# Making the decayed inputs of a state-space scan on VectorE from PSUM instead of on GpSimd from SBUF

## Chip, cores, metric

The kernel runs on one core of a Trainium2 chip. The metric is the device time of one launch in microseconds; the time before is the median of three runs.

## What is computed

The reference is one block of two layers on 2048 tokens of width 512: a Mamba-2 layer (chunked state-space scan, 16 heads of 64 channels, state 128) and a mixture of 8 experts. The change touches only the scan. Cut to what matters, per chunk of tokens:

```python
xdt = xc * dtc[..., None]                       # x scaled by its time step, per head
CB = einsum('bclgn,bcsgn->bcgls', Cc, Bc)
Y_diag = einsum('bcgls,bgHcls,bcsgHp->bclgHp', CB, Lmat, xdt)
decay_states = exp(dA_cs[..., -1:] - dA_cs)     # per head and token
states = einsum('bcsgn,bgHcs,bcsgHp->bcgHpn', Bc, decay_states, xdt)
# then the carry over chunks, Y_off, gate, RMS norm, output projection
```

The product `decay_states * xdt` under the last einsum is what the kernel calls `xdd`.

## The kernel before

The kernel has three stages on all engines: a front (router, decays; up to about 100 us), the experts, and, from about 285 us, the scan. The scan works on 16 tiles of 128 tokens, t = 0 to 15, in 8 groups of two tiles. Here an even tile is the first of its group (`c == 0`), an odd tile the second. Beside the tiles of group g, the engines compute the input projection, convolution and gate of group g + 1 in nine slices (`stage_pe`, `stage_act`, `stage_dve`), of which four lie in the even tile and five in the odd one. The last group (tiles 14 and 15) has no such slices beside it. All engines run a program in fixed order and meet by semaphores.

What a tile does, in the order of each engine:

- **TensorE** transposes B into `pk` (line 1631) and x into `pxb[0]`, `pxb[1]` (line 1635; each 128x512), multiplies C by B (`pk`, line 1639), runs the output projection of the tile before (`po`, line 1595), then the column sum of its squares (`pk`, line 1600, which waits for the third step of GpSimd's sum), then `py` from the carry (line 1616), the diagonal product `py<-m,xdt` (line 1623), and the new state `pxb<-xdd,btok` (line 1657), which waits for `xdd`. Slices of the next group (`pi`, line 1343) lie in between.
- **VectorE** makes `xdt` from the transposed x in PSUM, in two halves (line 1496), `cbm` (line 1503, after TensorE's line 1639), multiplies the decay kernel `m` by it (line 1506, 128x2048), then computes `cst` and `dec` of the next tile (lines 1446 and 1449), the residual (lines 1546 to 1555), convolution taps (line 1299), `var`, the products with `e` (line 1469), `y` (line 1478) and the carry (line 1535).
- **ScalarE** takes exponentials of `dec` and `cd` (lines 1362, 1363) as soon as VectorE's `dec` is there; behind them in its order stand a quarter of the next decay kernel (line 1370) and the squares of the finished tile (line 1386).
- **GpSimd** makes `xdd` from `xdt` and `dec` (line 1228), sums the squares of the tile before in three steps (lines 1208, 1210, 1212, after ScalarE's squares), issues two gathers (lines 1236, 1241), makes `rstdy` (line 1218), scales the carry (line 1249), and adds and gates `y` (lines 1254, 1257).

`xdd` is made in GpSimd's order directly ahead of the sum of squares:

```python
pool.wait_ge(xdt_done, t * 2 + 2 + CR)
pool.wait_ge(dec_done, t + 1 + CR)
pool.wait_ge(st, t + CR)
pool.tensor_tensor(xdd[:, :, :, :], xdt[:, :, :, :], dec[c]..., ALU.mult).then_inc(xdd_done, 1)
```

Of the kernel before, what the change touches and what calls it, by code (L numbers as in the profile page):

```python
# [18 lines left out]
ALU = mybir.AluOpType  # L19
# [8 lines left out]
P = 128  # L28
TOKENS, D = 2048, 512
KD = D // P  # L30
INNER, STATE, HEADS, HD, TAPS = 1024, 128, 16, 64, 4
XB = INNER // P
# [3 lines left out]
T = TOKENS // P  # L36
# [103 lines left out]
CR = 1  # L140
# [43 lines left out]
def static(i, *values):  # L184
    return isinstance(i, int) and i in values
# [754 lines left out]
def mamba(nc, low, over, late, wraw, whl, wo, xh0, smalls, hooks, sem, x, w_in, w_out_in, conv_w_in, conv_b_in,  # L940
# [5 lines left out]
    with ExitStack() as ctx:  # L946
        def pb(name, shape):
            return ctx.enter_context(nc.psum_tensor(name, shape, F32))
# [3 lines left out]
        xdt = over("xdt", [P, XB, 2, HD])  # L952
        xdd = over("xdd", [P, XB, 2, HD])
# [12 lines left out]
        dec = [late(f"dec{i}", [P, HEADS]) for i in range(2)]  # L966
        cd = [late(f"cd{i}", [P, HEADS]) for i in range(2)]
        var = late("var", [P, 1])
        rstd = late("rstdy", [P, 1])
        pwt = late("pwt", [P, 2])  # L970
        sidx = late("sidx", [P, 2], U32)
        carry = low("carry", [P, XB, 2, HD])
        e2 = low("e2", [P, XB, P])
# [7 lines left out]
        pxb = [pb(f"pxb{i}", [P, 4, P]) for i in range(2)]  # L981
# [18 lines left out]
        res_in = sem("res_in")  # L1000
        ya_in = [sem(f"ya_in{i}") for i in range(2)]
        sidx_done = sem("sidx_done")
        sidx_ready = sem("sidx_ready")
        pw_done = sem("pw_done")
        ra_done = sem("ra_done")
# [3 lines left out]
        inz_free = sem("inz_free")  # L1009
        halo = sem("halo")  # L1010
        tap = sem("tap")
        ctap = sem("ctap")
        txd = sem("txd")
        xs_done = sem("xs_done")
# [3 lines left out]
        xdt_done = sem("xdt_done")  # L1018
        cst_done = sem("cst_done")
        dsub = sem("dsub")  # L1020
        dec_done = sem("dec_done")
# [4 lines left out]
        cbm_done = sem("cbm_done")  # L1026
        m_done = sem("m_done")
        xdd_done = sem("xdd_done")
        st = sem("st")
        yoff = sem("yoff")  # L1030
        ydiag = sem("ydiag")
        ye = sem("ye")
        yd = sem("yd")
        cdec = sem("cdec")
        cadd = sem("cadd")
        yadd = sem("yadd")
        ygate = sem("ygate")
# [6 lines left out]
        var_done = sem("var_done")  # L1044
        rstd_done = sem("rstd_done_m")
        res_done = sem("res_done")
        o_done = sem("o_done")
# [83 lines left out]
        def groups(eng, body):  # L1131

            by_twos(eng, G, lambda g, par, r: body(g, par))
# [56 lines left out]
            sp.wait_ge(o_out, 16 * T + 16)  # L1190

        def gpsimd(pool):
            for s in (yadd, ygate, xdd_done, cdec, rstd_done):
                pool.sem_inc(s, CR)
            pool.sem_inc(tree, 3)
            pool.memset(nhalf[:, :], -0.5).then_inc(nh_done, 1)
            pool.wait_ge(nh_done, 1)
            pool.wait_ge(down, J + CR)
            pool.wait_ge(y_done, J + CR)
            pool.wait_ge(h_lo, J + 2)  # L1200
            pool.wait_ge(w_lo, NP)
            for i in range(2):
                pool.wait_ge(y_out[i], 16 * ((J + 1 - i) // 2) + 16)

            def sums(t):

                pool.wait_ge(ysqd, t + 1 + CR)
                pool.tensor_tensor(ysq[:, 0:4, :], ysq[:, 0:4, :], ysq[:, 4:8, :], ALU.add).then_inc(tree, 1)  # L1208
                pool.wait_ge(tree, t * 3 + 4)
                pool.tensor_tensor(ysq[:, 0:2, :], ysq[:, 0:2, :], ysq[:, 2:4, :], ALU.add).then_inc(tree, 1)  # L1210
                pool.wait_ge(tree, t * 3 + 5)
                pool.tensor_tensor(ysq[:, 0:1, :], ysq[:, 0:1, :], ysq[:, 1:2, :], ALU.add).then_inc(tree, 1)

            def factor(t):

                pool.wait_ge(var_done, t + 1 + CR)
                pool.wait_ge(o_done, t + CR)
                pool.tensor_tensor(rstd[:, :], var[:, :], nhalf[:, :], ALU.pow).then_inc(rstd_done, 1)

            def body(g, par):  # L1220
                for c in range(2):
                    t = g * 2 + c
                    first = static(t, 0)
                    if not static(t, T - 1):
                        pool.wait_ge(xdt_done, t * 2 + 2 + CR)
                        pool.wait_ge(dec_done, t + 1 + CR)
                        pool.wait_ge(st, t + CR)
                        pool.tensor_tensor(xdd[:, :, :, :], xdt[:, :, :, :],  # L1228
                                           dec[c][:, :].rearrange("p (a b) -> p b a", a=2).unsqueeze(3)
                                           .broadcast_to([P, XB, 2, HD]), ALU.mult).then_inc(xdd_done, 1)  # L1230
                    if not first:
                        sums(t - 1)

                    if not first:
                        pool.wait_ge(res_done, t + CR)
                    pool.tensor_copy(sidx[:, :], slot_u[:, :, bass.ds(t, 1)].rearrange("p k t -> p (k t)")  # L1236
                                     ).then_inc(sidx_done, 1)
                    pool.wait_ge(sidx_done, t + 1)
                    pool.sem_inc(sidx_ready, 1)
                    for n in range(2):  # L1240
                        pool.indirect_dma_start(ya[n][:, :], None, y_d, bass.IndirectOffsetOnAxis(ap=sidx[:, n:n + 1], axis=0)  # L1241
                                                ).then_inc(ya_in[n], 16)
                    if not first:
                        factor(t - 1)
                    if static(t, T - 1):
                        return
                    pool.wait_ge(yoff, t * 2 + 2 + CR)
                    pool.wait_ge(cadd, t * 2 + CR)
                    pool.tensor_tensor(carry[:, :, :, :], carry[:, :, :, :],
                                       cd[c][:, :].rearrange("p (a b) -> p b a", a=2).unsqueeze(3)  # L1250
                                       .broadcast_to([P, XB, 2, HD]), ALU.mult).then_inc(cdec, 1)
                    pool.wait_ge(yd, t * 2 + 2 + CR)
                    pool.wait_ge(ye, t * 2 + 2 + CR)
                    pool.tensor_tensor(y[:, :, :], y[:, :, :], e2[:, :, :], ALU.add).then_inc(yadd, 1)  # L1254
                    pool.wait_ge(yadd, t + 1 + CR)
                    pool.wait_ge(inz_free, g * NZ + NZ + CR)
                    pool.tensor_tensor(y[:, :, :], y[:, :, :], zs[par][:, :, c * P:(c + 1) * P],  # L1257
                                       ALU.mult).then_inc(ygate, 1)

            groups(pool, body)  # L1260
            sums(T - 1)
            factor(T - 1)
# [164 lines left out]
            square(T - 1)  # L1427

        def vector(dve):
            for s in (inz_free, xs_done, xdt_done, cbm_done, m_done, ye, yd, cadd, var_done, o_done, ctap, res_done):  # L1430
                dve.sem_inc(s, CR)
            dve.sem_inc(o_out, 16)
            for n in LAST:
# [23 lines left out]
            def body(g, par):  # L1457
                for c in range(2):
                    t = g * 2 + c
# [34 lines left out]
                    for half in range(2):  # L1494
                        dve.wait_ge(xtr, t * 2 + half + 1)
                        dve.tensor_tensor(  # L1496
                            xdt[:, 4 * half:4 * half + 4, :, :],
                            pxb[half][:, :, :].rearrange("p b (a d) -> p b a d", a=2),
                            dt_tok[:, bass.ds(t, 1), :].rearrange("p t (a b) -> p (t b) a", a=2)
                            [:, 4 * half:4 * half + 4, :].unsqueeze(3).broadcast_to([P, 4, 2, HD]),  # L1500
                            ALU.mult).then_inc(xdt_done, 1)
                    dve.wait_ge(cbt, t + 1)
                    dve.tensor_tensor(cbm[:, :], pk[:, 1, :], tri[:, :], ALU.mult).then_inc(cbm_done, 1)
                    dve.wait_ge(me, t + 1 + CR)
# [58 lines left out]
            def finish(t):  # L1563
# [6 lines left out]
                                         op0=ALU.mult, op1=ALU.add).then_inc(o_done, 1)  # L1570

            groups(dve, body)
            residual(T - 1)
            variance(T - 1)
            finish(T - 1)

        def tensor(pe):
# [88 lines left out]
            project(T - 1)  # L1666

        return {"sync": sync, "gpsimd": gpsimd, "scalar": scalar, "vector": vector, "tensor": tensor}


# [51 lines left out]
```

## Time and profile before

| | before |
|---|---|
| median of 3 runs | 766.76 us (764.72 to 768.8) |
| the profiled execution, its own time | 762.99 us |
| its span, first to last instruction | 760.9 us |
| TensorE busy | 657.8 us (86%) |
| VectorE busy | 513.5 us (67%) |
| ScalarE busy | 376.9 us (50%) |
| GpSimd busy | 329.8 us (43%) |
| mean granted TensorE clock | 0.971 |

Busy shares are over the whole span, three stages with different limits; what an edit is worth has to be read in the stretch in which it lies. The span leaves out some 2 us of the execution's own time at its two ends. Start times in the rows are counted from the span's start. "Idle before, releaser" says how long the engine stood ahead of an instruction and what ended that.

### The profile page before, as it was taken

How to read it: one execution, taken by the hardware profiler on the slowest of the kernel's cores; microseconds unless marked ns; L12 is line 12 of the kernel's file. 1: busy time of each engine (PE TensorE's matmuls, PEld its weight loads, DVE VectorE, ACT ScalarE, POOL GpSimd, SP SyncE). 2: the span in 40 equal slices, each digit the busy share in tenths (PEclk: the TensorE clock that was granted, in tenths of full speed). 3: DMA queues.
4: the chain of work that ended last, by engine and by line, in shares of the span. 5: the costliest groups of instructions: out<-in, count | busy, mean ns of one | idle time of the engine just before them, and what ended most of it. 6: DMA issues, size and time to landing. Idle time of an engine off the chain costs nothing.

```text
span 760.9 us, 13663 instructions
## 1 busy us (share of the span) xinstructions
PE 657.8 (86%) x4201; PEld 542.1 (71%) x4202; DVE 513.5 (67%) x987; ACT 376.9 (50%) x773; POOL 329.8 (43%) x305
## 2 busy tenths in 40 slices
PE   3970139999999988789999999999999999999765
PEld 3970128898998778776786786787777777777442
DVE  7339474434444467588788788788788787797464
ACT  1243313444544465767456556556555565654410
POOL 4208952223222100235564564555546546546451
PEclk9999959999999998999999999999999999999898
DMA  9992024644655613321342343243233233224121
GB/s 317 369 393 102 1 62 134 200 140 122 174 168 168 250 56 139 97 79 61 112 139 65 103 139 96 70 137 110 69 124 110 82 111 113 68 96 138 56 61 36
DMA packets 36062, 96.39 MB, mean 127 GB/s; under 512 B 5376, under 2 KB 9216, under 8 KB 33856
## 3 DMA queue, kind: packets, MB, share of 16 engines
q1 hardware_dynamic: 28304, 67.96, 25.8%
q0 software_dynamic: 7728, 28.05, 13.0%
q8 instruction: 16, 0.26, 0.1%
q14 instruction: 14, 0.11, 0.1%
HBM read 73.06 MB, written 22.94 MB: 126 GB/s over the span
## 4 chain that ended last, share of the span: by engine, by line
PE 58%; POOL 14%; issue 12%; DVE 8%; ACT 3%; DMA 3%; SPq 0%; POOLq 0%; DVEq 0%; ACTq 0%
PE pi L1343 19%; PE pg L877 9%; PE pd L888 6%; PE po L1595 5%; PE py L1616 4%; PE prt L648 3%; PE py L1623 3%; PE px L862 2%; POOL y L1254 2%; DVE y L1478 2%; PE pt L642 2%; POOL ysq L1208 2%; PE pxb L1657 2%; POOL xdd L1228 2%; DVE xs L1299 2%
## 5 line engine op out<-in xcount | busy, mean ns | idle before, releaser
L1343 PE MATMUL pi<-xh,whl 128*128 128x256 f32 x1152 | 166.9, 288 | 9.0 <-ACT raw L1274 4.6
L1343 PEld LDWEIGHTS pi<-xh,whl 128*128 128x128 f32 x1152 | 148.3, 191 | 13.4 <-issue 7.1
L1299 DVE SCALAR_TENSOR_TENSOR xs<-raw,conv_w,xs 128x256 f32<-128x256 f32 x240 | 119.6, 567 | 4.1 <-ACT xs L1277 4.1
L1595 PE MATMUL po<-wo,y 128*128 128x512 f32 x256 | 114.6, 601 | 1.4 <-POOL y L1257 0.9
L1343 PE MATMUL pi<-xl,whl 128*128 128x256 f32 x576 | 92.9, 284 | 0.0
L1595 PEld LDWEIGHTS po<-wo,y 128*128 128x128 f32 x256 | 48.3, 194 | 56.7 <-issue 55.3
L1370 ACT ACTIVATE m<-m,cst 128x128 f32<-128x128 f32 x256 | 79.4, 388 | 0.5
L1343 PEld LDWEIGHTS pi<-xl,whl 128*128 128x128 f32 x576 | 79.0, 191 | 0.0
L877 PE MATMUL pg<-ew,xgh 128*128 x312 | 65.3, 352 | 0.0
L1254 POOL TENSOR_TENSOR y<-y,e 128x1024 f32<-128x1024 f32 x15 | 35.8, 2388 | 65.2 <-DVE y L1478 65.2
L1208 POOL TENSOR_TENSOR ysq<-ysq 128x512 f32<-128x512 f32 x16 | 22.8, 1423 | 86.8 <-ACT ysq L1386 79.7
L1228 POOL TENSOR_TENSOR xdd<-xdt,dec 128x1024 f32<-128x1024 f32 x15 | 29.1, 1939 | 64.8 <-DVE xdt L1496 64.8
L877 PEld LDWEIGHTS pg<-ew,xgh 128*128 128x128 f32 x312 | 53.6, 192 | 0.1
L769 POOL DMA_INDIRECT xg<-xn_d,ic x39 | 38.9, 998 | 30.7 <-POOL ic L766 30.7
L1280 ACT ACTIVATE zs<-pi 128x512 f32<-128x512 f32 x32 | 19.1, 598 | 63.2 <-PE pi L1343 63.2
L1506 DVE TENSOR_TENSOR m<-m,cbm 128x2048 f32<-128x2048 f32 x16 | 47.6, 2976 | 1.7
L1241 POOL DMA_INDIRECT ya<-y_d,sidx x32 | 40.2, 1257 | 18.0 <-POOL sidx L1236 13.1
L888 PE MATMUL pd<-ew,hh 96*128 x156 | 45.9, 416 | 0.5 <-issue 0.5
L831 DVE SCALAR_TENSOR_TENSOR hg<-th,pg 128x192 f32<-128x192 f32 x39 | 13.8, 353 | 46.7 <-ACT th L789 46.7
L1277 ACT ACTIVATE xs<-raw,conv_b,conv_w 128x256 f32<-128x256 f32 x80 | 43.8, 594 | 1.3
L766 POOL COPY ic<-idx 128x1 uint32 (+1 forms) x39 | 9.2, 237 | 80.5 <-PE px L862 80.5
L840 DVE TENSOR_TENSOR hl<-ph,hh 96x256 fp32r<-96x256 f32 x39 | 16.4, 421 | 38.1 <-ACT hh L795 21.2
(180 smaller groups left out, 1278.6 us busy)
## 6 DMA issues: line engine op xcount, KB each, us to landing
m<-cs_d SPq DMA_DIRECT2D x16, 1024.0 KB, 4.7
y_d<-yo SPq DMA_DIRECT2D x39, 256.0 KB
e<-cs_d SPq DMA_DIRECT2D x32, 256.0 KB, 4.0
ew<-in_w_gu POOLq DMA_DIRECT2D x8, 768.0 KB, 16.1
xin<-in_x SPq DMA_DIRECT2D x8, 512.0 KB, 7.2
xn_d<-xin SPq DMA_DIRECT2D x8, 512.0 KB, 23.2
xt_d<-ew SPq DMA_DIRECT2D x8, 512.0 KB, 17.2
xl<-xt_d SPq DMA_DIRECT2D x8, 512.0 KB, 4.0
```

The lines of the kernel that those rows point to most:

```text
L769: pool.indirect_dma_start(xg[par][:, :], None, xn_d, bass.IndirectOffsetOnAxis(ap=ic[par][:, 0:1], axis=0)).then_inc(xg_in[par], 16)
L877: mm = pe.matmul(pg[par][:, :], xx[par][:, k, :], of(ww, e, k), start=n == 0, stop=n == 11)
L888: mm = pe.matmul(pd[par][:, :], xx[par][:, k, :], of(ww, e, k), start=n == 0, stop=n == 5)
L1228: pool.tensor_tensor(xdd[:, :, :, :], xdt[:, :, :, :], dec[c][:, :].rearrange("p (a b) -> p b a", a=2).unsqueeze(3) .broadcast_to([P, XB, ...
L1241: pool.indirect_dma_start(ya[n][:, :], None, y_d, bass.IndirectOffsetOnAxis(ap=sidx[:, n:n + 1], axis=0)).then_inc(ya_in[n], 16)
L1254: pool.tensor_tensor(y[:, :, :], y[:, :, :], e2[:, :, :], ALU.add).then_inc(yadd, 1)
L1277: act.activation(xs[par][:, b, :], raw[:, b, 0:GT], ACT.Identity, bias=conv_b[:, b:b + 1], scale=conv_w[:, b, 0:1]).then_inc(tap, 1)
L1299: dve.scalar_tensor_tensor(out=xs[par][:, b, :], in0=raw[:, b, k:k + GT], scalar=conv_w[:, b, k:k + 1], in1=xs[par][:, b, :], op0=ALU.mult ...
L1343: mm = pe.matmul(pi[n % 2][:, h, :], whl[:, n, lo, k, h * P:(h + 1) * P], xx[:, k, :], start=k3 == 0, stop=k3 == 11)
L1370: act.activation(m[c][:, h, :], m[c][:, h, :], ACT.Relu, bias=cst[c][:, h:h + 1], scale=-1.0).then_inc(seg, 1)
L1506: dve.tensor_tensor(m[c][:, :, :], m[c][:, :, :], cbm[:, :].unsqueeze(1).broadcast_to([P, HEADS, P]), ALU.mult).then_inc(m_done, 1)
L1595: mm = pe.matmul(po[:, :], y[:, b, :], wo[:, b, :], start=b == 0, stop=b == XB - 1)
```

## The change

The factor `dtd` (128x16) is `dec` times the time step, made by one small VectorE instruction. `xdd` is then the transposed x in PSUM times `dtd`, in two instructions of 128x512 on VectorE, between `xdt` and `cbm`. GpSimd's multiplication goes, and with it its three waits. The products are made for tiles 0 to 14, as before. VectorE now waits for ScalarE's `dec` of this tile (`dec_done`) and for its own `dtd` (`dtd_done`).

```diff
@@ gpsimd
-                    if not static(t, T - 1):
-                        pool.wait_ge(xdt_done, t * 2 + 2 + CR)
-                        pool.wait_ge(dec_done, t + 1 + CR)
-                        pool.wait_ge(st, t + CR)
-                        pool.tensor_tensor(xdd[:, :, :, :], xdt[:, :, :, :],
-                                           dec[c][:, :].rearrange("p (a b) -> p b a", a=2).unsqueeze(3)
-                                           .broadcast_to([P, XB, 2, HD]), ALU.mult).then_inc(xdd_done, 1)
@@ vector, after the two xdt instructions
+                    if not static(t, T - 1):
+                        dve.wait_ge(dec_done, t + 1 + CR)
+                        dve.tensor_tensor(dtd[:, :], dec[c][:, :], dt_tok[:, bass.ds(t, 1), :].rearrange("p t h -> p (t h)"),
+                                          ALU.mult).then_inc(dtd_done, 1)
+                        dve.wait_ge(dtd_done, t + 1)
+                        for half in range(2):
+                            ins = dve.tensor_tensor(
+                                xdd[:, 4 * half:4 * half + 4, :, :],
+                                pxb[half][:, :, :].rearrange("p b (a d) -> p b a d", a=2),
+                                dtd[:, :].rearrange("p (a b) -> p b a", a=2)
+                                [:, 4 * half:4 * half + 4, :].unsqueeze(3).broadcast_to([P, 4, 2, HD]), ALU.mult)
+                        ins.then_inc(xdd_done, 1)
                     dve.wait_ge(cbt, t + 1)
                     dve.tensor_tensor(cbm[:, :], pk[:, 1, :], tri[:, :], ALU.mult).then_inc(cbm_done, 1)
```

On VectorE, in the loop's odd tile, before (`pxb0`, `pxb1` are the halves of the transposed x, `m1` is this tile's decay kernel; ISA and REGISTER_ALU carry waits and counters):

```order
L1493 ISA
L1496 REGISTER_ALU [waits xtr_m,ydiag]
L1496 TENSOR_TENSOR xdt_146<-pxb0,dt_tok_52 128x512
L1495 REGISTER_ALU
L1496 ISA [waits xtr_m]
L1496 TENSOR_TENSOR xdt_146<-pxb1,dt_tok_52 128x512
L1503 TENSOR_TENSOR cbm_158<-pk,tri_50 128x128 [waits cbt]
L1504 REGISTER_ALU
L1506 TENSOR_TENSOR m1_145<-m1_145,cbm_158 128x2048 [waits cbm_done,me]
L1442 ISA
L1446 ISA [waits xdd_done,me,bc_in0]
```

and now:

```order
L1491 TENSOR_TENSOR xdt_146<-pxb0,dt_tok_52 128x512
L1490 REGISTER_ALU
L1491 ISA [waits xtr_m]
L1491 TENSOR_TENSOR xdt_146<-pxb1,dt_tok_52 128x512
L1498 REGISTER_ALU
L1499 TENSOR_TENSOR dtd_168<-dec1_162,dt_tok_52 128x16 [waits dec_done]
L1503 TENSOR_TENSOR xdd_147<-pxb0,dtd_168 128x512 [waits dtd_done]
L1503 TENSOR_TENSOR xdd_147<-pxb1,dtd_168 128x512
L1510 TENSOR_TENSOR cbm_158<-pk,tri_50 128x128 [waits cbt]
L1513 TENSOR_TENSOR m1_145<-m1_145,cbm_158 128x2048 [waits cbm_done,me]
L1437 ISA
L1441 ISA [waits xdd_done,me,bc_in0]
```

Three instructions came between the second `xdt` and `cbm`, so `cbm`, `m`, `cst` and `dec` all stand behind them.

On GpSimd, in the loop, from the gate of an even tile (`zs1`) to the sum of squares in the odd tile behind it, before:

```order
L1256 ISA [waits yadd]
L1257 TENSOR_TENSOR y_148<-y_148,zs1_156 128x1024 [waits inz_free]
L1225 ISA
L1226 REGISTER_ALU [waits xdt_done]
L1228 TENSOR_TENSOR xdd_147<-xdt_146,dec1_162 128x1024 [waits st,dec_done]
L1208 TENSOR_TENSOR ysq_149<-ysq_149 128x512 [waits ysqd]
L1209 ISA
L1210 TENSOR_TENSOR ysq_149<-ysq_149 128x256 [waits tree]
```

and now:

```order
L1251 ISA [waits yadd]
L1252 TENSOR_TENSOR y_148<-y_148,zs1_156 128x1024 [waits inz_free]
L1210 TENSOR_TENSOR ysq_149<-ysq_149 128x512 [waits ysqd]
L1211 ISA
L1212 TENSOR_TENSOR ysq_149<-ysq_149 128x256 [waits tree]
L1213 REGISTER_ALU
L1214 TENSOR_TENSOR ysq_149<-ysq_149 128x128 [waits tree]
```

The multiplication has gone from this place, and the sum of squares follows the gate directly.

## Rows read from the trace of the kernel before

**Rows 1.** The page: busy time of each engine, and slices of the span.

```profile
PE 657.8 (86%) x4201; PEld 542.1 (71%) x4202; DVE 513.5 (67%) x987; ACT 376.9 (50%) x773; POOL 329.8 (43%) x305
...
PE   3970139999999988789999999999999999999765
```

**Rows 2.** Who waited for whom, 320 to 700 us: total us, times, longest us.

```profile
PEld pk L1600 <- POOL ysq L1212: 7.0, 7, 1.0
```

**Rows 3.** Timeline of TensorE, tile 5 (odd), then tile 6 (even): start, us.

```profile
455.94 7.03 PE L1595 MATMUL po<-wo,y 128*128 128x512 f32 x16
463.17 0.38 PE L1600 MATMUL pk<-ones,ysq 128*128 128x1 f32 x2 [0.20 <-POOL ysq L1212]
463.41 1.14 PE L1616 MATMUL py<-xs,carry 128*128 128x128 f32 x8
...
485.47 7.03 PE L1595 MATMUL po<-wo,y 128*128 128x512 f32 x16
492.33 0.28 PE L1600 MATMUL pk<-ones,ysq 128*128 128x1 f32 x2
492.48 1.14 PE L1616 MATMUL py<-xs,carry 128*128 128x128 f32 x8
```

**Rows 4.** Timeline of VectorE in tile 5 (odd).

```profile
450.82 1.27 DVE L1496 TENSOR_TENSOR xdt<-pxb,dt_tok 128x512 f32<-128x512 f32 x2
453.31 0.29 DVE L1503 TENSOR_TENSOR cbm<-pk,tri 128x128 f32<-128x128 f32 x1 [1.22 <-PE pk L1639]
453.71 3.49 DVE L1506 TENSOR_TENSOR m<-m,cbm 128x2048 f32<-128x2048 f32 x1
457.13 0.16 DVE L1446 COPY cst<-cs_tok 128x16 f32 x1
457.32 0.18 DVE L1449 TENSOR_TENSOR dec<-m,cst 128x16 f32<-128x16 f32 x1
...
457.80 0.75 DVE L1551 SCALAR_TENSOR_TENSOR res<-ya,pwt,res 128x512 f32<-128x512 f32 x1 [0.20 <-DVE pwt L1546]
```

**Rows 5.** Timeline of GpSimd in the same tile.

```profile
450.52 2.63 POOL L1257 TENSOR_TENSOR y<-y,zs 128x1024 f32<-128x1024 f32 x1 [0.17 <-POOL y L1254]
453.12 1.93 POOL L1228 TENSOR_TENSOR xdd<-xdt,dec 128x1024 f32<-128x1024 f32 x1
460.21 1.45 POOL L1208 TENSOR_TENSOR ysq<-ysq 128x512 f32<-128x512 f32 x1 [5.16 <-ACT ysq L1386]
```

**Rows 6.** Timeline of VectorE, then GpSimd, in tile 6 (even).

```profile
479.44 1.29 DVE L1496 TENSOR_TENSOR xdt<-pxb,dt_tok 128x512 f32<-128x512 f32 x2
482.82 0.29 DVE L1503 TENSOR_TENSOR cbm<-pk,tri 128x128 f32<-128x128 f32 x1 [2.09 <-PE pk L1639]
483.22 2.29 DVE L1506 TENSOR_TENSOR m<-m,cbm 128x2048 f32<-128x2048 f32 x1
485.43 0.17 DVE L1446 COPY cst<-cs_tok 128x16 f32 x1
...
480.98 1.94 POOL L1228 TENSOR_TENSOR xdd<-xdt,dec 128x1024 f32<-128x1024 f32 x1 [1.21 <-DVE xdt L1496]
```

**Rows 7.** Timeline of tile 14: VectorE, GpSimd, and TensorE's wait.

```profile
701.97 1.28 DVE L1496 TENSOR_TENSOR xdt<-pxb,dt_tok 128x512 f32<-128x512 f32 x2
703.17 0.28 DVE L1503 TENSOR_TENSOR cbm<-pk,tri 128x128 f32<-128x128 f32 x1
703.55 3.86 DVE L1506 TENSOR_TENSOR m<-m,cbm 128x2048 f32<-128x2048 f32 x1
707.33 0.16 DVE L1446 COPY cst<-cs_tok 128x16 f32<-128x16 f32 x1
...
703.33 1.93 POOL L1228 TENSOR_TENSOR xdd<-xdt,dec 128x1024 f32<-128x1024 f32 x1 [0.90 <-DVE xdt L1496]
...
713.07 0.59 PE L1600 MATMUL pk<-ones,ysq 128*128 128x1 f32 x2 [3.45 <-POOL ysq L1212]
```

**Rows 8.** Timeline of VectorE in tile 0.

```profile
319.59 0.29 DVE L1503 TENSOR_TENSOR cbm<-pk,tri 128x128 f32<-128x128 f32 x1 [4.91 <-PE pk L1639]
```

More of the change, by code:

```diff
@@ L970, in mamba @@
         pwt = late("pwt", [P, 2])
+        dtd = late("dtd", [P, HEADS])
         sidx = late("sidx", [P, 2], U32)
@@ L1002, in mamba @@
         sidx_done = sem("sidx_done")
+        dtd_done = sem("dtd_done")
         sidx_ready = sem("sidx_ready")
@@ L1192, in gpsimd @@
         def gpsimd(pool):
-            for s in (yadd, ygate, xdd_done, cdec, rstd_done):
+            for s in (yadd, ygate, cdec, rstd_done):
                 pool.sem_inc(s, CR)
@@ L1429, in vector @@
         def vector(dve):
-            for s in (inz_free, xs_done, xdt_done, cbm_done, m_done, ye, yd, cadd, var_done, o_done, ctap, res_done):
+            for s in (inz_free, xs_done, xdt_done, xdd_done, cbm_done, m_done, ye, yd, cadd, var_done, o_done, ctap, res_done):
                 dve.sem_inc(s, CR)
```

## The prediction

> **What bounds the kernel now.** I read the page first. TensorE is busy 86% of the span, and in its slices nearly every one of the scan is a 9 [rows 1]: in the scan the time is TensorE's own work, and another engine counts only where TensorE waits for it. So the second view is who waited for whom. One of its lines bears on this change [rows 2]: TensorE's weight load at line 1600 waits for GpSimd's sum of squares, 7 times in 380 us and up to 1.0 us. No line of that view names `xdd` as what TensorE waited for.
>
> The third view is the timeline, tile by tile. In even tiles line 1600 starts 6.86 us after line 1595; in odd tiles 7.23 us, and the next product another 0.24 us later instead of 0.15 us [rows 3]. So an odd tile loses 0.37 + 0.09 = 0.46 us to the sum of squares and an even tile nothing. There are 7 odd tiles with a next group beside them (1 to 13). The chain to this wait runs: VectorE `xdt`, `cbm`, `m`, `cst`, `dec`, then ScalarE `dec`, a quarter kernel, squares, then GpSimd's three sums, then line 1600. GpSimd stood 5.16 us ahead of the sum in the odd tile [rows 5]. So GpSimd's time for `xdd` is not what holds that chain; when VectorE reaches `cst` is. I measure the change by the start of `cst`.
>
> **How GpSimd acts on VectorE.** `m` takes 2.29 us in tile 6 and 3.49 us in tile 5 [rows 4, 6]. In tile 5 GpSimd's `xdd` had begun at 453.12, before `m` at 453.71, and ended at 455.05; `m` ended 2.15 us later, nearly its whole undisturbed length [rows 4, 5]. In tile 14 `xdd` ended at 705.26 and `m` at 707.41, again 2.15 us later [rows 7]. So `m`, whose two inputs lie in SBUF, did nothing until GpSimd's instruction ended. A held instruction thus ends its own length less 0.14 us after the release. `xdt`, with one input in PSUM, takes 1.27 us for its two beside GpSimd's gate in tile 5 and 1.29 us mostly without it in tile 6 [rows 4 to 6]: it isn't held. VectorE also has a hole where the new work goes: 1.22 us of waiting for TensorE before `cbm` in tile 5, 2.09 us in tile 6.
>
> **The change part by part.** *Removed:* GpSimd's `xdd`, 15 of 1.93 or 1.94 us each [rows 5, 6], 29 us of busy time. In odd tiles it hides in the 5.16 us wait, so its own time is worth nothing. Its indirect cost is what it does to `m`: 3.49 - 2.29 = 1.20 us in each odd tile, 3.86 - 2.29 = 1.57 us in tile 14, nothing in even tiles, where it ends at 482.92, before `m` [rows 6]. GpSimd's waits that go had long been met, or stood in the same cover.
>
> *Added on VectorE:* `dtd`, like the `dec` of line 1449 0.18 us; then a wait for its own result, 0.20 us as ahead of `res` [rows 4]; then two `xdd` of the form of `xdt`, after which VectorE is free 1.20 us later (as `cbm` follows `xdt` in tile 14) [rows 7]. That is 1.58 us in 15 tiles, 24 us of busy and waiting time. The wait for `dec_done` costs nothing: ScalarE had made this `dec` in the tile before. The longer wait of TensorE for `xdd` doesn't arise either, since the product at line 1657 comes many us later.
>
> *Even tiles.* `xdt` begins at 479.44, so `dtd` can begin at 480.64, when GpSimd's gate has been over since 480.98 - 1.21 = 479.77. `xdd` begins at 481.02 and VectorE is free at 482.22, before `cbm` starts at 482.82 on TensorE's word [rows 6]. The cover is left with 0.60 us. `m` was not held before and is not now. Cost zero; without this cover it would be 1.58 us a tile.
>
> *Odd tiles.* `xdt` begins at 450.82, so `dtd` can begin at 452.02. But GpSimd's gate `y<-y,zs` runs until 453.15 [rows 4, 5], and `dtd` has two inputs in SBUF, `dec` and `dt_tok`. If it is held as `m` was, it ends between 453.15 + 0.04 and 453.15 + 0.18. `xdd` then begins at 453.39 to 453.53, `cbm` at 454.59 to 454.73 in place of 453.31, `m` 0.40 us later at 454.99 to 455.13, now undisturbed, and `cst` 2.21 us later [rows 6] at 457.20 to 457.34. Before, it began at 457.13. So an odd tile loses 0.07 to 0.21 us: the 1.2 us that `m` gets back are spent on the delay of `cbm`. No row shows an instruction as small as `dtd` beside GpSimd. The other end is that it isn't held: `xdd` at 452.40, `cbm` at 453.60, `m` at 454.00, `cst` at 456.21, 0.92 us earlier than before. I take the held case, middle 0.14 us, since `m`, the only instruction with two SBUF inputs in these rows that met GpSimd at work, was held in both places to the very end of GpSimd's instruction.
>
> The Trainium skill says in "SBUF — State Buffer", section "Who interferes with whom", that a VectorE instruction with two SBUF inputs contends with a GpSimd instruction that reads SBUF, and that the one that comes first has the shared interface to its end. The rows of `m` agree, with the 2.15 us. By this rule, which speaks against the change, the odd tile loses 0.07 to 0.21 us; by the row of `dec` alone, 0.18 us long with GpSimd idle, it would gain.
>
> *Tile 14* has no slice of a next group, and TensorE waits 3.45 us there for the same sum [rows 7], so this chain sets the end. `xdt` begins at 701.97, `dtd` at 703.17; GpSimd's gate ended at 703.33 - 0.90 = 702.43, so nothing holds it. `xdd` at 703.55, `cbm` at 704.75 (TensorE's product is there already), `m` at 705.15, `cst` at 707.36, against 707.33. So +0.03 us: 1.57 us given back, 1.58 us paid. Tile 15 makes no `xdd`. In tile 0 VectorE waits 4.91 us for TensorE ahead of `cbm` [rows 8], three times what is added: nothing.
>
> **Sum.** 7 x 0.14 + 0.03 = 1.0 us, between 7 x 0.07 + 0.03 = 0.5 us and 7 x 0.21 + 0.03 = 1.5 us. The profiled execution's own 763.0 us becomes 764.0 us. It lay 3.8 us under the median, inside the spread of the runs (764.7 to 768.8) but for 1.7 us; on the median the same sum gives 766.8 + 1.0 = 767.8 us. About 0.5%, 3.8 us, is what a measurement of this kernel can tell from no change.
>
> **Rivals.**
> *A, `dtd` is not held by GpSimd.* Then `cst` comes 0.92 us earlier in odd tiles, the sum of squares too, and TensorE's 0.46 us wait in seven tiles is gone; the rest of the 0.92 us has nobody waiting for it. 7 x 0.46 = 3.2 us less: 763.6 us on the median. For it speaks that `dtd` reads only 16 elements a partition. Against it, that `m` made no headway at all while held.
>
> *B, `m` stays long.* If what stretches `m` in odd tiles is not `xdd` on GpSimd but another engine's traffic at that time (ScalarE, or the transfer of `e`), the new work is paid and nothing comes back: in odd tiles 0.14 + 1.20 = 1.34 us, in tile 14 1.57 + 0.03 = 1.60 us, in all 11.0 us, 777.8 us on the median. The point from which it decides is a loss of half a microsecond per odd tile, where the total passes 3.8 us. For it: the added work is VectorE's, whose chain TensorE waits for already. Against it: `m` ended 2.15 us after `xdd` in two places with different neighbours, and was undisturbed where `xdd` was over.
>
> *C, the freed GpSimd lets everything come forward.* If the sum of squares had waited behind `xdd`, 1.9 us would go from the chain. The 5.16 us of idleness between them [rows 5] leaves this no room, and I give it nothing.
>
> **How the numbers follow.** Forecast 0.65, A 0.2, B 0.07; 0.08 is left for a loss or gain that I have not named, equally on both sides. The range starts at 763.0 us, A with the spread's share, and ends at 771.5 us: the upper end of the sum, 768.3 us, plus half the spread of the runs (2 us), with a little of B's smaller sizes. B in full and part of the unnamed are left out. Faster by over 0.5%: 0.12 (part of A, half the unnamed). Slower by over 0.5%: 0.11 (B, half the unnamed). Within 0.5%: 0.77.
>
> **What would show it.** Right: GpSimd's busy time falls by 29 us, VectorE's grows by only some 10 us (about 22 us of new instructions less 7 x 1.20 + 1.57 of `m`); `m` takes 2.29 us in all tiles but 15; `dtd` in odd tiles takes over 1 us, ending with GpSimd's gate, and 0.18 us in even tiles; `cbm` in odd tiles no longer waits for TensorE; the wait at line 1600 is there in odd tiles and 0.1 us longer. `dtd` at 0.18 us in odd tiles and no wait there means A. `m` at 3.4 us means B. A new wait of TensorE for `xdd` at line 1657, or `xdd` slower than `xdt`, would prove the costs wrong.

## The result and the profile after

| | before | changed |
|---|---|---|
| median of 20 runs each | 764.74 us (761.91 to 768.80) | 769.20 us (764.61 to 775.01) |
| ratio | 1 | 1.0054, 95% interval 1.0035 to 1.0073 |
| the profiled execution, its own time | 762.99 us | 770.32 us |
| its span | 760.9 us | 768.2 us |

The changed kernel is slower by some 4.1 us (2.7 to 5.6). The forecast was 1.0 us slower, between 0.5 and 1.5. On the forecast's base the ratio makes 766.8 x 1.0054 = 770.9 us, inside the stated range of 763.0 to 771.5, but the sum missed most of the loss. The loss is about the 0.5% that was named as the least that can be told from no change; the interval reaches to both sides of it.

The page of the kernel after, engines' busy time, slices, and the two queues that bring instructions:

```profile
PE 661.1 (86%) x4201; PEld 545.0 (71%) x4202; DVE 530.6 (69%) x1032; ACT 376.9 (49%) x773; POOL 300.3 (39%) x290
...
PE   3970139999999879789999999899999899999775
...
q8 instruction: 16, 0.26, 0.1%
q14 instruction: 24, 0.20, 0.1%
```

GpSimd lost 29.5 us of busy time and VectorE gained 17.1 us [rows 1]. TensorE's row now has an 8 in the middle of its nines in two places that had none. The last line, `q14`, had 14 packets and 0.11 MB before: ten more packets of instructions.

Who waited for whom after, 320 to 700 us, the lines that are new or changed against [rows 2]:

```profile
PEld pk L1607 <- POOL ysq L1214: 12.2, 9, 3.1
...
DVE xdt L1491 <- issue: 7.9, 2, 4.1
...
PE pk L1607 <- POOL ysq L1214: 4.6, 4, 2.3
```

(Line 1607 is the old 1600, line 1491 the old 1496, line 1214 the old 1212.) VectorE stood 7.9 us ahead of `xdt` for nothing that the profile shows, in two pieces. The timeline says where (start, length, engine, line, and in brackets the idle time ahead and what ended it). The kernel after, VectorE in tile 6:

```profile
478.84 0.69 DVE L1300 SCALAR_TENSOR_TENSOR zs<-zs,pi 128x512 f32<-128x512 f32 x1 [2.08 <-ACT zs L1275]
483.64 1.29 DVE L1491 TENSOR_TENSOR xdt<-pxb,dt_tok 128x512 f32<-128x512 f32 x2 [4.11 <-issue]
484.85 0.17 DVE L1499 TENSOR_TENSOR dtd<-dec,dt_tok 128x16 f32<-128x16 f32 x1
485.05 1.29 DVE L1503 TENSOR_TENSOR xdd<-pxb,dtd 128x512 f32<-128x512 f32 x2
```

The same stretch on TensorE:

```profile
485.61 7.03 PE L1602 MATMUL po<-wo,y 128*128 128x512 f32 x16
494.91 0.58 PE L1607 MATMUL pk<-ones,ysq 128*128 128x1 f32 x2 [2.27 <-POOL ysq L1214]
495.35 2.06 PE L1623 MATMUL py<-xs,carry 128*128 128x128 f32 x8
```

The last transpose of x had started at 478.9, and VectorE had finished `zs` at 479.53, about where `xdt` began before [rows 6]. It came 4.11 us later, and the whole chain behind it with it, so that TensorE waited 2.27 us for the sum of squares in an even tile, where it had not waited at all [rows 3]. The second such wait is 3.81 us at the start of tile 10. Tiles 2, 6 and 10 are where the three passes of VectorE's scan loop begin, so the waits lie at the two branches back.

The odd tile on VectorE, after, answers to [rows 4]:

```profile
450.96 1.27 DVE L1491 TENSOR_TENSOR xdt<-pxb,dt_tok 128x512 f32<-128x512 f32 x2
452.16 1.26 DVE L1499 TENSOR_TENSOR dtd<-dec,dt_tok 128x16 f32<-128x16 f32 x1
453.45 1.29 DVE L1503 TENSOR_TENSOR xdd<-pxb,dtd 128x512 f32<-128x512 f32 x2
454.66 0.28 DVE L1510 TENSOR_TENSOR cbm<-pk,tri 128x128 f32<-128x128 f32 x1
455.05 2.29 DVE L1513 TENSOR_TENSOR m<-m,cbm 128x2048 f32<-128x2048 f32 x1
457.25 0.17 DVE L1441 COPY cst<-cs_tok 128x16 f32 x1
```

And GpSimd's gate in it, which answers to [rows 5]:

```profile
450.98 2.41 POOL L1252 TENSOR_TENSOR y<-y,zs 128x1024 f32<-128x1024 f32 x1 [0.50 <-POOL y L1249]
```

`dtd` takes 1.26 us for 16 elements and ends at 453.42, 0.03 us behind GpSimd's gate; `m` is undisturbed. All of this is as forecast, but for the wait of 0.20 us behind `dtd`, which was 0.03.

To split the loss by place, this is the length of single tiles, from one start of TensorE's transpose of B to the next in the timelines (us):

| tile | 5 (odd) | 6 (even) | 9 (odd) | 10 (even) | 13 (odd) | 14 |
|---|---|---|---|---|---|---|
| before | 29.37 | 26.34 | 29.36 | 26.34 | 29.38 | 22.37 |
| after | 29.37 | 30.38 | 29.30 | 30.09 | 29.31 | 22.11 |

In the profiled executions tiles 6 and 10 cost 4.04 + 3.75 = 7.8 us. All the other tiles together gave back 0.9 us, and the scan began 0.5 us later. That accounts for the 7.3 us between the spans to within 0.1 us. The medians lie 4.5 us apart: the two profiled executions differ by more than that, and why is taken up at the end of the experiments.

### The profile page after: what moved, and what is told of

The parts are those of the page before. It is cut to its first block, busy times and chain, and to the rows that moved or that the text cites. A ratio compares the mean times of both kernels' runs of the same rounds, so it can differ in the third digit from the quotient of the medians.

```text
span 768.2 us, 13683 instructions
## 1 busy us (share of the span) xinstructions
PE 661.1 (86%) x4201; PEld 545.0 (71%) x4202; DVE 530.6 (69%) x1032; ACT 376.9 (49%) x773; POOL 300.3 (39%) x290
## 4 chain that ended last, share of the span: by engine, by line
PE 56%; issue 18%; POOL 12%; DVE 7%; ACT 3%; DMA 3%; POOLq 0%; SPq 0%; DVEq 0%; ACTq 0%
PE pi L1338 17%; PE pg L877 9%; PE pd L888 6%; PE po L1602 6%; PE py L1623 4%; PE prt L648 3%; PE px L862 2%; PE pt L642 2%; PE py L1630 2%; POOL ysq L1210 2%; POOL y L1249 2%; DMA xg<-xn_d,ic 1%; POOL y L1252 1%; POOL sp L369 1%; PE pxb L1664 1%
## 5 line engine op out<-in xcount | busy, mean ns | idle before, releaser
L1338 PEld LDWEIGHTS pi<-xh,whl 128*128 128x128 f32 x1152 | 150.0, 194 | 13.4 <-issue 7.1
L1244 POOL TENSOR_TENSOR carry<-carry,cd 128x1024 f32<-128x1024 f32 x15 | 29.0, 1934 | 56.3 <-PE py L1623 56.3
L1269 ACT COPY raw<-pi 128x512 f32<-128x512 f32 x40 | 23.1, 578 | 37.7 <-PE pi L1338 37.4
L1623 PE MATMUL py<-xs,carry 128*128 128x128 f32 x256 | 39.1, 301 | 2.4 <-DVE e L1464 2.4
```

Source lines behind the costliest of these rows:

```text
L1338: mm = pe.matmul(pi[n % 2][:, h, :], whl[:, n, lo, k, h * P:(h + 1) * P], xx[:, k, :], start=k3 == 0, stop=k3 == 11)
L1623: mm = pe.matmul(py[0][:, b, :], cols, xs[par][:, XB + 1, tok], start=True, stop=True)
```

## The experiments

Ratios and times are against the kernel before, run beside each experiment; brackets give the 95% interval. Code is cut to the lines that matter.

Two theories for the two waits. **C**, code placement: at the branch back VectorE has to fetch the loop's first instructions again, depending on where the loop lies in its program. **W**: the wait belongs to the added work. In the built program the loop runs from instruction 364 to 703 of VectorE before, and from 371 to 722 after (the second number is the one that follows its last instruction).

**1. Longer code, no other work (b_pad19).** In the kernel before, ahead of VectorE's line 611:

```diff
+            for _ in range(19):
+                dve.sem_inc(spare, 1)
             dve.wait_ge(tok_done, 1)
```

> The kernel before with 19 semaphore increments that nobody reads added on VectorE in the front, where it waits about 10 us for TensorE (ahead of its line 611); not one instruction of the scan is changed. In the built program VectorE's scan loop, 339 instructions long, then ends after instruction 722 as in the changed kernel, instead of after 703. Theory C (code placement: the wait of some 4 us that VectorE has at the loop's two branches back, for nothing the profile shows, comes from fetching the loop's first instructions again, and depends on where the loop lies): the same two waits appear here at the start of tiles 6 and 10, TensorE then waits 2 us or more each time at the sum of squares, and the time rises by 4 to 7.5 us, ratio 1.005 to 1.010. Theory W (the wait belongs to the added work: dtd, its semaphores or the xdd pair): no such wait, ratio 1.000 within 0.001.

Measured: 1.0101 (1.0073 to 1.0129), 772.73 us. VectorE's wait in the view of who waited for whom (us in total, times, longest us), 320 to 700 us:

```profile
DVE xdt L1499 <- issue: 7.5, 2, 3.7
```

Its timeline of VectorE in tile 6:

```profile
483.85 1.29 DVE L1499 TENSOR_TENSOR xdt<-pxb,dt_tok 128x512 f32<-128x512 f32 x2 [3.72 <-issue]
485.05 0.28 DVE L1506 TENSOR_TENSOR cbm<-pk,tri 128x128 f32<-128x128 f32 x1
485.44 4.03 DVE L1509 TENSOR_TENSOR m<-m,cbm 128x2048 f32<-128x2048 f32 x1
```

Theory W falls: with not one instruction of the scan changed, 19 increments ahead of it bring both waits. The ratio came out just above the expected range. GpSimd's `xdd` is still there: started late by the late `xdt`, it now holds `m` in this tile too, 4.03 us in place of 2.29. Yet tiles 6 and 10, 30.39 and 30.37 us long, are hardly longer than in the changed kernel (30.38 and 30.09). Of the 3.7 us by which this profiled span is longer than that of the changed kernel, 1.5 us lie in tile 14 (23.64 against 22.11 us), where the granted clock was 0.50 from 720.9 to 731.1 us; in the changed kernel it was so from 720.1 to 726.9 us. What makes that stretch longer is not shown: it was as long again in run 3, where GpSimd makes no `xdd`.

**2. Where the limit lies (b_pad10).** The same with 10 increments.

> The kernel before with 10 idle increments in place of 19; its loop ends after instruction 713, between 703 (no wait) and 722 (wait). Theory C leaves both open: waits of some 4 us in tiles 6 and 10 put the limit at 704 to 713, none at 714 to 722.

Measured: one run, 772.91 us, with both waits. VectorE's waits in the same view:

```profile
DVE xdt L1499 <- issue: 7.4, 2, 3.7
```

So the loop from 364 to 703 goes free and the one from 374 to 713 pays.

**3. The changed kernel, its loop moved far back (a_pad150).** 150 increments in the same place.

> The changed kernel with 150 such increments in the same idle place; the loop of 351 instructions then runs from 521 to 872 of the built program. Theory C: both waits at the branch back are gone, everything else is as in the changed kernel, and the time is that of the kernel before within 1 us (ratio 0.999 to 1.001), as the odd tiles' cst came neither earlier nor later. Theory W: the waits stay, ratio 1.005.

Measured: 1.0041 (1.0024 to 1.0058), 767.76 us. VectorE's waits over the whole span:

```profile
DVE tokf L614 <- issue: 12.1, 1, 12.1
DVE xdt L1494 <- issue: 7.5, 2, 3.8
```

TensorE in its tile 6:

```profile
491.71 0.38 PE L1610 MATMUL pk<-ones,ysq 128*128 128x1 f32 x2 [1.97 <-POOL ysq L1217]
491.95 1.14 PE L1626 MATMUL py<-xs,carry 128*128 128x128 f32 x8
```

A miss: the waits stayed. I had taken a loop from 521 to 872 to be placed well; it isn't, and it too contains the instructions from 703 to 713. Also, 150 increments don't fit into the 10.2 us of waiting there, which became 12.1 us. What the run did show is under the clock below: its tiles 6 and 10 lose only 2.2 and 2.1 us, though VectorE's waits are about as long.

**4. `dtd` a tile ahead, same padding (a_early_pad150).** `dtd` of tile t + 1 is made behind the residual in tile t, and ahead of the tile's products VectorE only waits for its own count. `factors` waits for `dec_done` and `xdd_done` and multiplies `dec` by `dt_tok` into `dtd`:

```diff
+                    if not static(t, T - 1, T - 2):
+                        factors(t + 1, 1 - c)
                     for n in taken[:2]:
```

> As the run before, but dtd of the next tile is made right behind the residual, when GpSimd stands idle, so that GpSimd's gate can't hold it; in the odd tiles xdd then follows xdt at once. If the hold of dtd is what eats the gain, cst in odd tiles comes 1.0 to 1.2 us earlier than in the kernel before, TensorE's 0.46 us wait at the sum of squares in seven odd tiles is gone, and tile 14 gains 0.2 to 0.4 us: 3 to 4 us less than before, ratio 0.995 to 0.996. If TensorE has another wait right behind it, the ratio is 0.998 to 1.000.

Measured: 1.0006 (0.9990 to 1.0023), 765.04 us, with both waits at the branch back, whose absence this forecast took for granted. The part on the hold came true. VectorE in its tile 5:

```profile
449.38 1.27 DVE L1501 TENSOR_TENSOR xdt<-pxb,dt_tok 128x512 f32<-128x512 f32 x2
450.58 1.27 DVE L1512 TENSOR_TENSOR xdd<-pxb,dtd 128x512 f32<-128x512 f32 x2
...
454.48 0.17 DVE L1444 COPY cst<-cs_tok 128x16 f32 x1
```

From the start of `xdt` to the start of `cst` it is 5.10 us, where it was 457.13 - 450.82 = 6.31 us [rows 4]. `xdd` starts right behind `xdt`, and tile 5 is 28.90 us long in place of 29.37.

**5. GpSimd's `xdd` alone taken away (b_xdd_first_only).** From tile 1 on the kernel before leaves out the product, and GpSimd's three waits with it. So this run prices the product and is no version to use:

```diff
-                    if not static(t, T - 1):
+                    if not static(t, 0, T - 1):
+                        pool.sem_inc(xdd_done, 1)
+                    elif static(t, 0):
```

> The kernel before with GpSimd's multiplication made in tile 0 alone; tiles 1 to 14 use tile 0's xdd, so the states are left out of the computation from there on. Nothing is added on VectorE. This measures what GpSimd's xdd costs by holding m: m at 2.29 us in all tiles but 15, cst 1.2 us earlier in odd tiles, TensorE's wait there gone (7 x 0.46 = 3.2 us) and 1.57 us less in tile 14: 4.8 us less, ratio 0.994. If the stretched m has another cause, m stays at 3.4 us and the ratio is 1.000.

Measured: 0.9918 (0.9894 to 0.9942), 759.20 us. All of `m` by its line (durations in ns, min/median/max, then the first and last start):

```profile
L1508 DVE TENSOR_TENSOR m<-m,cbm x16: 2292/2292/3395, 321.3 to 724.8; 128x2048 f32<-128x2048 f32 x16
```

TensorE in its tile 5:

```profile
456.45 7.03 PE L1597 MATMUL po<-wo,y 128*128 128x512 f32 x16
463.32 0.28 PE L1602 MATMUL pk<-ones,ysq 128*128 128x1 f32 x2
```

`m` is undisturbed in all tiles but 15, and line 1602 comes 6.87 us behind line 1597 where it was 7.23 us [rows 3]. The seven odd tiles are 0.39 to 0.49 us shorter, 3.1 us in all (tile 5: 28.90 us), and tile 14 1.26 us. So `xdd` on GpSimd did cost the kernel time, by holding `m`: the whole change had 4.3 us to win by the tiles, if the products had been free, and 6.3 us (4.4 to 8.1) by the ratio.

**6. Control (b_sp).** VectorE primes 19 semaphores ahead of experts and scan (20 in the changed kernel, which adds that of `xdd_done`). These increments are moved to SyncE's front, and the loop then runs from 345 to 684:

```diff
-                dve.sem_inc(s, CR)
@@ front, sync, ahead of store_xn(0)
+            for s, n in front.biases:
+                sp.sem_inc(s, n)
```

> The kernel before, with the 20 increments by which VectorE primes its semaphores ahead of the experts and the scan moved to SyncE's front, where it waits for VectorE. VectorE's scan loop then ends after instruction 684 of the built program in place of 703. A control for the two runs that follow: no wait at the branch back, ratio 0.998 to 1.000.

Measured: 0.9989 (0.9973 to 1.0004), 762.88 us, no wait at the branch back. The move itself is worth nothing that the interval can tell.

**7. The changed kernel with the same move (a_sp).** Its loop runs from 351 to 702.

> The changed kernel with the same 20 increments moved; its loop of 351 instructions then ends after 702 instead of 722, one less than in the kernel before. Theory C (where the loop ends decides): both waits of some 4 us at the branch back are gone, odd tiles as in the changed kernel (dtd held, TensorE's wait at the sum of squares as before), ratio to the kernel before 0.998 to 1.001, and equal to that of the control within 0.001. Theory L (the length of the loop, 351 against 339, decides, not its place): the waits stay, ratio 1.005 or more.

Measured: 0.9992 (0.9977 to 1.0006), 763.39 us. No line "xdt <- issue" is left. Its page, the queue of instructions:

```profile
q14 instruction: 14, 0.11, 0.1%
```

The groups of `m` and `dtd` by line (busy us, mean ns, idle before):

```profile
L1507 DVE TENSOR_TENSOR m<-m,cbm 128x2048 f32<-128x2048 f32 x16 | 37.8, 2362 | 1.7
...
L1493 DVE TENSOR_TENSOR dtd<-dec,dt_tok 128x16 f32<-128x16 f32 x15 | 9.6, 637 | 0.0
```

TensorE in its tile 5:

```profile
462.73 0.38 PE L1601 MATMUL pk<-ones,ysq 128*128 128x1 f32 x2 [0.20 <-POOL ysq L1211]
```

The same 351 instructions in the loop, the same work, and the ten extra packets and the loss are gone: the loop's length is not what decides, its place is. What the change does apart from that is nothing that can be told from the control: tile 6 is 26.32 us, tile 5 29.35 us.

**8. Both costs removed (a_early_sp).** `dtd` made a tile ahead, the increments moved, and three waits left out that VectorE's own order already meets (`ydiag` ahead of `xdt`, `xdd_done` ahead of `cst` and of `dtd`), so that the loop runs from 350 to 701.

> dtd made a tile ahead, where GpSimd is idle, the 20 increments moved, and waits left out that VectorE's own order already meets; the loop is 351 instructions and ends after 701. Both costs of the change are gone if theory C is right: no wait at the branch back, no hold of dtd, no wait of TensorE for the sum of squares in odd tiles, 0.37 us gained in tile 14. 3 to 4.5 us less than before, ratio 0.994 to 0.996. If the waits at the branch back stay, 1.001 or more.

Measured: 0.9953 (0.9935 to 0.9970), 759.47 us. VectorE in its tile 5:

```profile
449.22 1.27 DVE L1489 TENSOR_TENSOR xdt<-pxb,dt_tok 128x512 f32<-128x512 f32 x2
450.42 1.27 DVE L1500 TENSOR_TENSOR xdd<-pxb,dtd 128x512 f32<-128x512 f32 x2
451.70 0.29 DVE L1507 TENSOR_TENSOR cbm<-pk,tri 128x128 f32<-128x128 f32 x1
452.10 2.29 DVE L1510 TENSOR_TENSOR m<-m,cbm 128x2048 f32<-128x2048 f32 x1
454.31 0.17 DVE L1434 COPY cst<-cs_tok 128x16 f32 x1
...
456.44 0.17 DVE L1442 TENSOR_TENSOR dtd<-dec,dt_tok 128x16 f32<-128x16 f32 x1
```

TensorE in the same tile:

```profile
454.33 7.03 PE L1601 MATMUL po<-wo,y 128*128 128x512 f32 x16
461.19 0.28 PE L1606 MATMUL pk<-ones,ysq 128*128 128x1 f32 x2
```

`dtd` is 0.17 us again, `xdd` follows `xdt` at once, and TensorE goes from line 1601 to line 1606 in 6.86 us. Its tile 5 is 28.90 us long, 0.47 us less than before. Run 4, which still had the waits on `ydiag` and `xdd_done`, has the same 28.90 us there, so it is the place of `dtd` that gains it and not the waits left out. This version beats both kernels.

The tile lengths of all of them (us), worked out as above:

| | tile 5 | tile 6 | tile 10 | tile 13 | ratio |
|---|---|---|---|---|---|
| before | 29.37 | 26.34 | 26.34 | 29.38 | 1 |
| changed | 29.37 | 30.38 | 30.09 | 29.31 | 1.0054 |
| b_pad19 | 29.39 | 30.39 | 30.37 | 29.37 | 1.0101 |
| b_pad10 | 29.37 | 30.38 | 30.36 | 29.39 | one run |
| a_pad150 | 29.38 | 28.56 | 28.46 | 29.28 | 1.0041 |
| a_early_pad150 | 28.90 | 29.98 | 28.41 | 28.90 | 1.0006 |
| b_xdd_first_only | 28.90 | 26.33 | 26.31 | 28.89 | 0.9918 |
| b_sp | 29.37 | 26.32 | 26.34 | 29.37 | 0.9989 |
| a_sp | 29.35 | 26.32 | 26.34 | 29.28 | 0.9992 |
| a_early_sp | 28.90 | 26.33 | 26.33 | 28.88 | 0.9953 |

**Whether code is fetched in the waits.** Counts of packets don't say when they moved, but the traces time each packet of `q14`. The five kernels with waits have ten of them, 3.7 to 4.1 us long. In every one, one packet of 8 KB starts 1.4 to 1.9 us after VectorE went idle (in tile 6 of the changed kernel at 481.39, in the wait from 479.53 to 483.64), and the next 0.3 to 0.5 us after VectorE went on. Between 460 and 620 us these kernels have 8 or 9 packets on that queue, and the five without waits none or one. So instructions do move in each wait, as theory C has it. That they are VectorE's is inferred from their coming only with its waits.

**What a late VectorE costs beyond TensorE's wait.** TensorE waits 2.27 us in tile 6 of the changed kernel, yet the tile is 4.04 us longer. The busy time and the granted clock by stretches (start:end, length, then the busy us of PE, PEld, DVE, ACT and POOL with their instructions, the clock, the DMA share and GB/s), in the changed kernel right behind that wait:

```profile
494.91:497.06 2.15, 2.15 (x10) 2.15 (x11) 2.15 (x7) 1.89 (x6) 1.33 (x2) 0.50 0.00 0
497.06:500.02 2.96, 2.96 (x22) 2.96 (x22) 2.16 (x6) 1.08 (x4) 2.15 (x3) 0.81 0.47 116
```

The changed kernel again, behind its wait in tile 10:

```profile
610.90:614.10 3.20, 3.20 (x17) 3.20 (x17) 2.80 (x7) 2.16 (x8) 2.86 (x3) 0.50 0.28 82
```

The same view of a_pad150, behind its wait of 1.97 us:

```profile
492.50:500.00 7.50, 7.50 (x64) 5.97 (x64) 6.53 (x17) 6.41 (x18) 5.15 (x4) 1.00 0.47 140
```

In the changed kernel TensorE resumed at half its clock (1.2 in place of 2.4 GHz) in both tiles, and eight `py` products took 2.06 us in place of 1.14; in a_pad150 it stayed at full clock, and the tile lost little more than the wait. a_early_pad150 has one of each: 3.64 us lost in tile 6, where the granted clock was 0.50 from 493.4 to 496.7 us, and 2.1 us in tile 10, where it was 1.00, with waits of 1.84 and 1.81 us. So each wait at the branch back costs about 2 us, or up to 4 us when the clock falls behind it, and from execution to execution of the changed kernel it need not be the same. The 20 executions of the changed kernel bear it out as far as they go: the three shortest spans (762.5 to 763.1 us) had a mean granted clock of 0.984 to 0.986, the five longest (768.4 to 772.9 us) 0.964 to 0.978. The 23 of the kernel before beside run 7 show no such order (759.5 us at 0.984, 760.2 us at 0.968, 765.8 us at 0.980). It may also be why the profiled executions lie further apart than the medians, but where in the span the clock was lower is known for the profiled one only.

## Why the prediction was right or wrong

**The view of the kernel was right.** TensorE is what bounds the scan, GpSimd's time for `xdd` was worth nothing by itself, and its cost lay in holding `m`. Run 5 measured that cost, forecast from rows as 4.8 us: the tiles show 3.1 + 1.26 = 4.3 us, and the ratio 6.3 us (4.4 to 8.1). Run 7, which has no `xdd` on GpSimd either, gains nothing from GpSimd's free time.

**The hold of `dtd`** was the step that I chose without a row for so small an instruction, and it was right: 1.26 us in odd tiles, 0.17 us in even ones, ending with GpSimd's gate. That is what the Trainium skill says in "SBUF — State Buffer", section "Who interferes with whom"; the trace agrees, with 16 elements too. Runs 7 and 8 show what followed from it: 0.9992 with the hold and 0.9953 without. Rival A fell, and its gain (3.2 us) is just what is had by moving `dtd` (7 x some 0.45 us).

**Even tiles 2, 4, 8 and 12** hid the added work, as forecast: `cbm` still started on TensorE's word.

**Some sizes were a little off.** The wait of VectorE for its own `dtd` was put at 0.20 us; `xdd` starts 0.03 us behind the end of `dtd`. The sum for an odd tile was 0.07 to 0.21 us of loss; it was 0.00 to 0.09 us of gain in the loop's tiles. Tile 14 was put at +0.03 us and came out at -0.26 us in the one trace; in run 7 against the control it is +0.12 us (22.36 against 22.24), so its sign is not settled. VectorE's busy time was to grow by 10 us and grew by 17.1 us. The prediction's own terms, about 22 less 10, make 12; the rest is the hold of `dtd`, which I forgot to count as busy, 7 x 1.1 = 7.7 us, and together that is somewhat too much.

**The step that failed** is the start of `xdt` in the even tiles, which the sum took over from the kernel before: "*Even tiles.* `xdt` begins at 479.44, so `dtd` can begin at 480.64", and from it "Cost zero; without this cover it would be 1.58 us a tile." In tile 6 itself, the one whose rows I had read, `xdt` began at 483.64, and tiles 6 and 10 cost 4.04 and 3.75 us. The sum counted the time of the added instructions and not their places in the program: a term for code was missing, and no rival stood for it. Seven instructions ahead of the loop and twelve in it moved the loop from 364 to 703 to 371 to 722, and there both branches back wait. That the measured time still lies in the stated range was luck: it is owed to the room left for the spread of the runs and for rival B, neither of which made the loss.

Without the waits the forecast of no change holds: run 7 has 0.9992 (0.9977 to 1.0006), where +1.0 us would be 1.0013, and its control has 0.9989. The sum was thus slightly too high, as the sizes above are. Rival B, the slower one, fell with `m` at 2.29 us in every tile but 15: the kernel was slower for another reason.

## What to carry to other kernels

An edit that adds instructions to an engine in a loop has two costs, their time and their place: before trusting a sum of durations, compare where the loop begins and ends in each engine's program with where it did, and look in the new trace for a wait "issue" at the first instruction behind the branch back. A loop that pays this can be cured without touching it, by moving or dropping instructions ahead of it; not just any other place will do, as run 3 shows. And when work leaves GpSimd for VectorE, a small helper with two SBUF inputs belongs where GpSimd is idle, since its length says nothing about how long it is held.

## What the runs showed of the hardware that was not expected

The wait at the branch back, 3.7 to 4.1 us, came with loops of 339, 351 and 359 instructions and stayed away with loops of 339 and 351. It was seen on VectorE alone; in the built program the scan loops of ScalarE and GpSimd have 224 and 84 instructions and TensorE's has 667, and no run moves those.

It came with the loops 371 to 722, 383 to 722, 374 to 713, 521 to 872 and 525 to 884, and not with 364 to 703, 345 to 684, 351 to 702 and 350 to 701. At least two readings fit all of these. By one the loops that wait are those that contain the instructions 704 to 713 of the built program. By the other they are those that begin behind a place between 364 and 371. Every run that moved the end moved the start with it, so none tells the two apart. The instruction queue moved 24 to 27 packets in place of 14 or 15 whenever the wait came.

The Trainium skill has a cause for it in "Runtime: NRT & Kernel Launch", section "Instruction fetch mechanics": instructions are held in blocks of 256, two at a time, and a taken branch to one that is no longer held waits for its transfer. The packets agree, and so do the runs with loops from 371, 374 and 383 on, if a block ends between 703 and 713: such a loop touches three blocks. The loops from 521 and 525 on would touch only two and waited all the same, so the rule of two blocks doesn't settle where a loop is safe; that stays open, as does what the loaded program has ahead of the built one.
